# The last three experts of layer 1 all add to the result, one after another, while the even sum is loaded

## The reference, cut to what matters

```
logits = h @ gate_w.T                       # h = layernorm(x), 4096 tokens
topk_w, topk_idx = top_k(softmax(logits), 4); topk_w /= sum(topk_w)
...                                         # tokens are sorted into slots of their experts, 256 per expert
gu = einsum('ech,ehi->eci', buf[:, :C], w_gate_up)
expert_out = einsum('eci,eih->ech', silu_and_mul(gu), w_down)
routed = zeros.at[t_s].add(expert_out[e_s, slot] * gate)
shared = silu_and_mul(h @ shared_w_gate_up) @ shared_w_down
x = x + tanh(g_ffn[1]) * (routed + shared)
```

## Time and profile before

| what | value |
|---|---|
| median of 3 runs | 1097.07 us (1092.88 to 1104.72) |
| the profiled execution | 1106.13 us, of which the span of its records 1104.1 us |
| PE busy over the span | 910.6 us (82%) |
| POOL busy over the span | 556.1 us (50%) |
| start of the last indirect addition | 1062.23 us |
| start of the first load of `acc_d` | 1062.24 us |
| start of the first merge | 1070.78 us |
| bytes moved by the DMA engines | 189.71 MB, mean 172 GB/s |

### The profile page before, as it was taken

The page is one execution under the profiler, slowest core; times in us unless marked ns, Lnnn a source line. Parts: engine busy times, 40 slices in busy tenths (PEclk is TensorE's granted clock), DMA queues, the critical chain, the costliest instruction groups (busy, mean ns, idle before and its releaser), DMA issues. The chain is left out here.

```text
span 1104.1 us, 18614 instructions
## 1 busy us (share of the span) xinstructions
PE 910.6 (82%) x5465; PEld 762.5 (69%) x5465; DVE 659.2 (60%) x2223; ACT 463.8 (42%) x1721; POOL 556.1 (50%) x592
## 2 busy tenths in 40 slices
PE   4988759999999698888548989999999979999910
PEld 3663437887877588777437888888888866888710
DVE  3603025766777465655448889999999973444431
ACT  1313652232322135544227677777677741222100
POOL 1300124455555625555543766666666653767861
PEclk8878988788988799999769999999999999999965
DMA  9521885668786967777399953523413005999689
GB/s 307 182 87 42 233 233 138 149 202 223 220 209 199 252 205 218 220 225 218 125 276 209 232 136 123 200 75 133 123 36 109 16 16 143 256 247 236 72 183 164
DMA packets 163957, 189.71 MB, mean 172 GB/s; under 512 B 16035, under 2 KB 145209, under 8 KB 163858
## 3 DMA queue, kind: packets, MB, share of 16 engines
q1 hardware_dynamic: 112882, 121.87, 38.1%
q0 software_dynamic: 33792, 46.46, 19.5%
q10 hardware_dynamic: 17184, 20.19, 5.3%
HBM read 96.19 MB, written 103.63 MB: 181 GB/s over the span
## 5 line engine op out<-in xcount | busy, mean ns | idle before, releaser
L1794 ACT ACTIVATE att<-bank,mx 128x77 f32<-128x77 f32 x512 | 159.4, 341 | 16.9 <-DVE mx L1875 16.1
L1742 POOL DMA_INDIRECT slots_d<-rows,place x128 | 128.2, 1002 | 71.8 <-DVE place L1963 40.6
L960 POOL DMA_INDIRECT y_d<-rows,targets x78 | 81.5, 1045 | 70.0 <-DVE rows L1291 48.3
L1794 ACT ACTIVATION_READ_ACCUMULATOR att<-bank,mx 128x1 f32 x512 | 114.5, 224 | 0.0
L2063 PE MATMUL bank<-vwo_hi,attT_hi 128*128 128x256 f32 x320 | 93.6, 292 | 2.9 <-DMA vwo_lo<-vwo_lo_d 2.1
L2064 PE MATMUL bank<-vwo_lo,attT_hi 128*128 128x256 f32 x320 | 90.7, 283 | 0.0
L2065 PE MATMUL bank<-vwo_hi,attT_lo 128*128 128x256 f32 x320 | 90.6, 283 | 0.0
L2063 PE MATMUL bank<-wqk_hi,xa_hi 128*128 128x462 f32 (+1 forms) x192 | 76.7, 400 | 6.1 <-DVE xa_lo L1880 5.0
L927 POOL DMA_INDIRECT slots_d<-rows,place x64 | 63.8, 997 | 15.9 <-issue 15.4
L1313 PE MATMUL bank<-wd_hi,act_hi 128*128 128x256 f32 (+1 forms) x206 | 69.9, 339 | 1.8 <-POOL act_lo L921 1.0
L1781 ACT ACTIVATE attT_hi<-bank 128x512 fp32r<-128x512 f32 x64 | 38.9, 609 | 77.2 <-PE bank L2104 77.2
(11 more groups left out here) (302 smaller groups left out, 2724.7 us busy)
## 6 DMA issues: line engine op xcount, KB each, us to landing
expert_gate_up<-in_wgu SPq DMA_DIRECT2D x40, 256.0 KB
rows<-slots_d SPq DMA_DIRECT2D x39, 260.0 KB
slots_d<-zrow SPq DMA_DIRECT2D x8, 1168.0 KB
expert_rows<-slots_d SPq DMA_DIRECT2D x32, 292.0 KB
x_res<-y_d POOLq DMA_DIRECT2D x14, 512.0 KB, 12.1
expert_down<-in_wd SPq DMA_DIRECT2D x40, 128.0 KB
wqk_d<-wqk SPq DMA_DIRECT2D x32, 154.0 KB, 3.6
vwo_d<-vwo SPq DMA_DIRECT2D x16, 308.0 KB
```

The costliest lines, as they stand in the source:

```text
L960: pool.indirect_dma_start(y0_d, bass.IndirectOffsetOnAxis(ap=tgt0[:, s % NY0, b:b + 1], axis=0), y_rows(s, b), None, bounds_check=T * K0 - ...
L1742: pool.indirect_dma_start(slots_d, bass.IndirectOffsetOnAxis(ap=place[:, n % 3, k:k + 1], axis=0), rows[:, n % 3, :], None, bounds_check=S ...
L1794: last = act.activation(att[:, par, h * S:(h + 1) * S], bank[:, a, i * S:(i + 1) * S], ACT.Exp, scale=-1.0, bias=mx[:, par, h:h + 1], accu ...
```

## The change

Before, the sum of an expert is chosen by e % 2, and the counts are written out as 16 experts each. After, it is chosen by a list, `goes_to`: even experts 0 to 28 go to `acc_d` (sum 0), odd ones to `result` (sum 1), and expert 30 goes to `result` as well. So experts 29, 30 and 31 all go to `result`. `adds_to(i, e)` counts the experts ahead of e that go to sum i, and takes the place of e // 2 and of E1 // 2 in the three waits. Sum 0 now has 15 experts and sum 1 has 17.

```diff
+            goes_to = [min(e % 2 + e // (E1 - 2), 1) for e in range(E1)]
+
+            def adds_to(i, e):
+                return sum(goes_to[g] == i for g in range(e))
...
-                    sp.wait_ge(added4[0], 16 * BLK * (E1 // 2))
+                    sp.wait_ge(added4[0], 16 * BLK * adds_to(0, E1))
...
                     for e in range(E1):
-                        total = (acc_d, out)[e % 2]
+                        i = goes_to[e]
+                        total = (acc_d, out)[i]
                         pool.wait_ge(g_y, e + 1)
-                        want(pool, added4[e % 2], 16 * BLK * (e // 2))
+                        want(pool, added4[i], 16 * BLK * adds_to(i, e))
                         for b in range(BLK):
                             pool.indirect_dma_start(
                                 total, bass.IndirectOffsetOnAxis(ap=target[:, e % NY, b:b + 1], axis=0),
                                 y[:, e % NY, b, :], None, bounds_check=T + BLK * P - 1, oob_is_err=True,
-                                compute_op=ALU.add).then_inc(added4[e % 2], 16)
-                    pool.wait_ge(added4[1], 16 * BLK * (E1 // 2))
+                                compute_op=ALU.add).then_inc(added4[i], 16)
+                    pool.wait_ge(added4[1], 16 * BLK * adds_to(1, E1))
```

## The result

The changed kernel takes 1106.87 us (median of 20 runs, 1099.29 to 1114.08), the kernel before on the same chip 1100.66 us (20 runs). The ratio is 1.0059 with a 95% interval of [1.0037, 1.0081]: slower by 4 to 9 us, inside the 1% named ahead, but clear of zero. The forecast was +2.4 us.

What follows compares the result with a forecast made beforehand. It took POOL's additions (one every 1.86 us), then DMA work, as the bound. First merge at 1077.9 plus 24.3 us gave 1102.2 against 1099.8: +2.4 us, 1108.5 profiled, forecast median 1099.5 us, range 1090 to 1107.

Steps and rivals of the forecast that it cites:

- the 1% named ahead: Whole kernel: about 1% (11 us) is what a measurement can tell from no change; chance 0.90 of landing within it.
- (b): Expert 29's second addition now meets SP's first load and lands after 8.55 us, at 1063.35; bounds 3.62 and 8.55.
- (c): Expert 30 waits for 29: starts at 1063.45, second half 1.86 us later, which lands 6.9 us after its start, at 1072.2.
- (d): Expert 31 waits for 30: starts at 1072.3, second half at 1074.15, no load left, lands 3.62 us later at 1077.8.
- (e): The merges: first starts at 1077.9, 7.1 us later than before; 24.3 us from there to the last landing, at 198 GB/s.
- (a): SP's loads start 7.5 us earlier, ending near 1070.8 instead of 1082.0; DVE's adds beside POOL's issues cost nothing.
- Rival 1: Loads are cheap for POOL's last additions: each lands after 3.62 us, -5.9 us, or 1091.2; chance 0.07.
- rival 2: Fair sharing of DMA engines: an addition's burst only doubles beside loads, 4.8 us to land; -2.9 us, or 1094.2; chance 0.23.
- rival 3: The chain of experts 29 to 31 stays in the loads, each landing after 8.55 us; +9.0 us, or 1106.0; chance 0.10.
- the two signs of being wrong: Merges alone run faster than 198 GB/s from the first packet, or additions to one tensor in a row land slower without loads.
- The chance of 0.60: Whole kernel: chance given to the prediction's own forecast, 1099.5 us, with its terms moved by a few tenths to 2 us.

Runs made afterwards that it cites:

- e1: Changed kernel, but DVE's eight adds of the loaded sum wait until expert 31 has landed; ratio 1.0046 to the kernel before.
- e2: Changed kernel without the loads of the even sum and DVE's adds of it, so even experts are missing from the result; ratio 0.9978 to the kernel before.
- e3: Changed kernel, but SP starts the loads only when expert 31 has landed; ratio 1.0095 to the kernel before.
- e6: Kernel before with parities swapped: even experts and 31 add to the result, other odd ones to the loaded sum; loads after 29; ratio 0.9999.
- e4: Changed kernel, but expert 30 adds to an unread third tensor and 31 waits for 29 alone; ratio 1.0040 to the kernel before, 0.9964 when run again.
- e8: Changed kernel, but its four loads of 1 MB each start only when the one ahead has landed; ratio 1.0044 to the kernel before.
- e5: Changed kernel, but the even sum is loaded in eight 512 KB parts, each started after the one ahead landed; ratio 1.0043 to the kernel before.
- e7: The swapped-parity kernel of e6, but with the load in eight parts, each started after the one ahead landed; ratio 1.0071 to the kernel before.
- e10: Kernel before, but its four loads each start only when the one ahead has landed; ratio 1.0049.
- e9: The swapped-parity kernel of e6, but its four loads each start only when the one ahead has landed; ratio 1.0043 to the kernel before.

## Why the prediction was wrong

The sum and the profile, in us from T0:

| step | forecast | changed kernel |
|---|---|---|
| (b) 29 lands | 8.55 | 8.56 |
| (c) from there to the start of 30 | 0.10 | 1.56 |
| (c) pair of 30 | 1.86 | 1.86 |
| (c) 30 lands | 6.9 | 5.73 |
| (d) from there to the start of 31 | 0.10 | 0.83 |
| (d) pair of 31 | 1.86 | 2.72 |
| (d) 31 lands | 3.62 | 3.84 |
| first merge | 0.10 | 0.29 |
| (e) from the first merge to the last landing | 24.3 | 25.5 |
| sum | 47.4 | 50.9 |

The step that failed is the size of three terms: POOL's start after a wait (c, d) was put at 0.1 us and took 1.56 and 0.83, DVE's adds beside POOL's issues (a) were put at nothing and cost 0.86, and the time from the first merge to the last landing (e) was put at 24.3 us and took 25.5. The mechanism was right. The loads move by as much as forecast (a), all but 11 of their packets have passed by T0 + 15.8 (forecast 1070.8, which is T0 + 16.0), the addition beside their start begins late and lands after 8.56 us as the row in the same position gave (b), and the engines stand idle while one expert waits for another. Rival 1 (3.62 us, cheap loads) and rival 2 (fair sharing, 4.8 us) are refuted by 8.56 and 8.18 us in the changed kernel and e1; rival 3 did not come, as the loads ran out before 31. The sign of the sum was right too. But it was called no change, and it is a change: +5.9 us by the tail where the sum gave +2.4. That 1106.87 still lies inside the range of 1090 to 1107 is luck: the upper end was there for rival 3, which did not come. Nor did either of the two signs of being wrong that the prediction named: the merges run at 197 GB/s (1096 to 1104), and additions in a row to one tensor land after 3.8 us without loads (e2).

The 3.5 us missing are sizes of terms.

**POOL's start after a real wait (c, d).** I took the 0.1 us from the 0.09 between a landing at 1054.71 and the addition at 1054.80, which the earlier trace rows lists as released by it. I misread it: the addition at 1054.80 is the second half of 29, behind no wait of its own. The wait met at 1054.71 is expert 30's (for 28), and 30 starts at 1056.66, 1.95 us later and on the usual pace of 1.86 us. The chain of waits of the kernel before, 1045 to 1104, has the stretch:

```profile
1054.71 0.02 issue
...
1054.80 0.03 POOLq L1756
1054.83 1.25 POOL result L1756
1056.07 0.58 issue
1056.66 1.55 POOL acc_d L1756
```

The queue's instructions lie beside the issue of 29's second half and so were covered. Uncovered they take 1.56 and 0.83 us, in e1 and e3 as well, and in e2 with nothing else going on (1.57 and 0.84). Of the 2.2 us added, 1.2 were absorbed at 30 (5.73 instead of 6.9): its packets came only as the loads ran out, so a later issue did not make them later. The rest stays. Why 30 pays 1.23 us of "issue" where 31 pays 0.50 is open. It does not come from the length of the wait: the 1.25 us above stand in the same place ahead of 30, and so do 1.23 us in e6 (at 1022.95), both beside the issue ahead.

**DVE's adds beside POOL's issues (a).** I took 0, from a bound of 0.6 us for each of two issues. e1 shows 0.86 us on the chain: with the adds held back, the pair of 31 is 1.86 us apart instead of 2.72.

**The merges' own start (e).** I counted a slow first stretch for the loads, 0.85 us, and none for the merges, since before they start inside a running load where it can't be seen. Alone they move 0.77 MB in their first 5 us instead of 0.96 to 0.99, which is about 1 us of the 1.2. e2 has the same 29.8 us without any load. What makes the start slow is open. So what the loads cost the merges, put at about 5 us, was 3.5 (33.3 - 29.8).

Two small slips changed little. In (c), 5.1 us after 1065.3 is 1070.4 and not 1070.6. And the burst of an addition is nearer 1.4 us than 1.15: the strip of the earlier trace rows ends at 1056.2 with packets still coming, and 35 more follow by about 1056.4. That would move rival 2 up by about 0.2 us for each addition and leaves the forecast as it is.

The chance of 0.60 on a spread of "a few tenths to 2 us" took the terms to err either way. The costs left out all had one sign; only the landing of 30 came out shorter.

## What to carry to other kernels

Before giving an earlier start to one stream by making another one serial, count the serial links as landing + restart + issue (here 3.8 + 0.8 to 1.6 + 1.86 us against 3.71 us for a pair in the pipeline), once with nothing beside them and once with the moved work beside them, and compare both with what the moved work had cost in its old place: here 1.9 and 9.4 us later, against 3.5 us gained. A wait that was always met early says nothing on what its engine needs to start again; take that price from a row where the engine really stood. And when DMA engines are the bound at the end, early work helps only if the last link is late by less than that gain.

## What the runs showed of the hardware

An addition of 128 rows that meets loads is late by more than its share of the engines: it lands 3.6 to 3.9 us after its issue alone, after 8.2 to 8.6 with 4 MB of loads started at the same time (both kernels, e1, e4, e6), after 7.9 with 1 MB (e8), and after 5.5 to 6.8 in the middle or at the end of a load (changed kernel, e1, e4, e6, e8). It is not the additions only: a load of 0.5 MB that takes 3.7 us takes 9.3 to 11.9 behind queued merges (e5, e7), one of 1 MB 12.2 or 13.7 instead of 5.4 (e10, e9).

The late start goes both ways between the two queues. e9's last load starts at 1069.70, and from then to 1073 the DMA queues have no packet of q1, merges only:

```profile
q0 software_dynamic: 564, 0.56, 124.5%
```

e5's last part starts at 1061.95, and from 1062 to 1066 only 5 of 800 packets are its own. So nearly all of its packets come 4 us or more after its start, where the loads of the kernel before had theirs after 1.6. What makes a transfer start late beside another queue's is not shown.
